# A window-attention block after a quantized convolution: spreading each head's softmax sum by a shuffle on VectorE in place of a product on TensorE

## What is computed

```python
attn = softmax(einsum('brqhd,brkhd->brhqk', qh, kh) * scale)
out  = einsum('brhqk,brkhd->brqhd', attn, vh)      # 8 channels of one head
x = x + out @ wo + bo
x = x + gelu(layernorm(x) @ w1 + bm1) @ w2 + bm2
```

## Time and profile before

| | |
|---|---|
| median of three runs | 5986.81 us (5982.99 to 5993.53) |
| profiled execution | 5993.37 us |
| its span, first to last instruction | 5991.5 us |
| PE, DVE, ACT, POOL busy | 82%, 61%, 55%, 46% |
| mean granted TensorE clock | 0.861 of full speed |

### The profile page before, as it was taken

How to read it: one execution, slowest core, us unless ns; L and a number is a source line. 1 busy time by engine, 2 the same in 40 slices (tenths; PEclk the granted TensorE clock), 3 DMA queues, 4 the chain that set the end, 5 groups by cost and what they waited for, 6 DMA issues and landing times.

```text
span 5991.5 us, 184263 instructions
## 1 busy us (share of the span) xinstructions
PE 4903.3 (82%) x43666; PEld 3154.2 (53%) x43666; DVE 3655.8 (61%) x8855; ACT 3301.0 (55%) x6282; POOL 2770.8 (46%) x9656
## 2 busy tenths in 40 slices
PE   3388888888888888888888888888887888888888
PEld 1265555545555455555555555555554555555564
DVE  2266665656656565665666666565665766656565
ACT  1156555565555655555565555655555565555646
POOL 1345444454544545444454544545444454544543
PEclk8588988989888898888888889798888989888869
DMA  2433332323323333342333323333332333323311
GB/s 64 99 91 79 88 102 61 99 73 97 88 70 106 75 88 78 86 104 60 98 74 96 90 75 100 76 88 79 86 101 64 99 73 99 88 70 102 77 24 32
DMA packets 626976, 494.17 MB, mean 82 GB/s; under 512 B 483792, under 2 KB 613968, under 8 KB 615536
## 3 DMA queue, kind: packets, MB, share of 16 engines
q10 hardware_dynamic: 335360, 212.04, 15.6%
q1 hardware_dynamic: 290416, 268.94, 15.5%
HBM read 268.80 MB, written 211.94 MB: 80 GB/s over the span
## 4 chain that ended last, share of the span: by engine, by line
PE 40%; POOL 14%; POOLq 14%; issue 14%; DMA 7%; DVE 4%; ACT 3%; DVEq 2%; ACTq 1%; SPq 1%
PE ps L984 10%; POOLq L223 9%; POOL vg L490 7%; PE ps L998 7%; PE ps L1014 6%; POOL kg L475 4%; PE ps L877 3%; DMA max_d<-tr 3%; POOLq L224 2%; POOL xin L502 2%; PE ps L897 2%; DMA qm<-qk_d 2%; DVEq L223 2%; PE ps L970 2%; PE ps L893 2%
## 5 line engine op out<-in xcount | busy, mean ns | idle before, releaser
L717 DVE TENSOR_REDUCE mx<-ps 128x4 f32<-128x1024 f32 x1568 | 1921.7, 1226 | 1763.7 <-PE ps L984 1550.6
L828 ACT ACTIVATE pt<-ps 128x512 f32<-128x512 f32 x3136 | 1695.8, 592 | 1228.5 <-PE ps L998 1145.7
L490 POOL COPY vg<-vs 64x72 f32 x6272 | 1544.2, 246 | 1396.6 <-POOL kg L475 1064.6
L984 PE MATMUL ps<-kg,qm 96*128 96x256 f32 x6272 | 1381.2, 348 | 642.5 <-POOL kg L475 224.0
L984 PEld LDWEIGHTS ps<-kg,qm 96*128 96x128 f32 x6272 | 996.3, 214 | 1437.1 <-issue 1191.2
L475 POOL CAST kg<-ks 96x128 fp32r x3136 | 858.3, 298 | 1560.5 <-POOL vg L490 926.9
L998 PE MATMUL ps<-qm,kg 97*128 97x256 f32 x6272 | 1160.0, 310 | 110.9 <-DMA qm<-max_d 56.2
L1014 PE MATMUL ps<-pt,vg 128*32 128x128 f32 x25088 | 1139.1, 304 | 38.2 <-DVE um L707 22.6
L998 PEld LDWEIGHTS ps<-qm,kg 97*128 97x128 f32 x6272 | 985.6, 215 | 156.8 <-ACT pt L828 92.5
L1014 PEld LDWEIGHTS ps<-pt,vg 128*32 128x32 f32 x25088 | 653.8, 118 | 293.1 <-issue 72.2
L626 DVE CAST kg<-ks 96x128 fp32r x3136 | 622.5, 240 | 131.7 <-issue 124.3
(11 more groups left out here) (113 smaller groups left out, 4083.8 us busy)
## 6 DMA issues: line engine op xcount, KB each, us to landing
qk_d<-stg SPq DMA_DIRECT2D x224, 448.0 KB, 3.6
qm<-qk_d ACTq DMA_DIRECT2D x1792, 42.0 KB
ks<-qk_d ACTq DMA_DIRECT2D x96, 784.0 KB, 6.2
vs<-v_d ACTq DMA_DIRECT2D x64, 882.0 KB, 7.1
xin<-in_x SPq DMA_DIRECT2D x119, 224.0 KB, 2.6
xi_d<-xi SPq DMA_DIRECT2D x112, 224.0 KB, 2.3
qk_d<-stg SPq DMA_DIRECT2D x112, 224.0 KB, 3.0
max_d<-tr SPq DMA_DIRECT2D x1568, 2.0 KB
```

The costliest lines, as they stand in the source:

```text
L490: j = pool.tensor_copy(vg[slot][rows, (k // 2) * VW:(k // 2 + 1) * VW], vs[place(m)[0]][rows, bass.ds(region, 1), :].rearrange("p o n -> p ...
L717: v.tensor_reduce(mx[h % 2][:].rearrange("p (g j e) -> p g j e", g=2, j=2)[:, :, :, 0], ps[:, 0:2, :].rearrange("p g (j k) -> p g j k", j= ...
L828: act.activation(pt[m % 2][:, c], ps[:, 2 + c, :], ACT.Exp, scale=float(HD) ** -0.5).then_inc(S["pt_ready"], 1)
L984: i = pe.matmul(ps[:, g, 256 * j:256 * j + 256], qm[c % 2][0:NP3, t, g, 2 * j:2 * j + 2, :].rearrange("p h t -> p (h t)"), kg[slot][0:NP3, ...
```

## The change

- `pick` and the products L934 go away.
- DVE shuffles instead, in `finish` at off 0 and off 1 of each strip: one STREAM_SHUFFLE of 128x448 each, which permutes rows within each group of 32. `SPREAD` gives row 16 to rows 0 to 7 and 17 to rows 8 to 15. It reads `um0`/`um1` and writes `rc`, both in on-chip memory (SBUF).
- The logarithm on ACT reads `rc` in place of the accumulators.
- PE's waits move: those that guarded banks 5 and 6 before L934 go to off 4 and off 9, or away.

```diff
--- before.py
+++ after.py
@@ -32,6 +32,8 @@
 VC = 18
 VW = 4 * VC
 
+SPREAD = [16] * HD + [17] * HD + [16] * 16
+
 
 
 
@@ -106,7 +108,6 @@
         max_d = dram("max_d", (RING, HEADS // 2, 128))
 
         ident = sb("ident", [128, 128])
-        pick = sb("pick", [128, 128])
         second = sb("second", [128, 1])
         parts = sb("parts", [128, 8])
         mean_w = sb("mean_w", [128, 128])
@@ -447,17 +448,11 @@
         def _(pool):
 
             Z = S["zero2"]
-            for i, t in enumerate((ident, pick)):
-                pool.memset(t[:], 0.0).then_inc(Z, 1)
-            pool.wait_ge(Z, 2)
+            pool.memset(ident[:], 0.0).then_inc(Z, 1)
+            pool.wait_ge(Z, 1)
             pool.affine_select(out=ident[:], in_=ident[:], compare_op=ALU.not_equal, fill=1.0, base=0,
                                pattern=[[-1, 128]], channel_multiplier=1).then_inc(Z, 1)
-            v = pick[:].rearrange("p (m b) -> p m b", m=4)
-            for e, span in ((0, slice(0, 8)), (1, slice(8, 16)), (0, slice(16, 32))):
-                w = span.stop - span.start
-                pool.affine_select(out=v[:, :, span], in_=v[:, :, span], compare_op=ALU.not_equal, fill=1.0, base=-16 - e,
-                                   pattern=[[-32, 4], [0, w]], channel_multiplier=1).then_inc(Z, 1)
-            pool.wait_ge(Z, 6)
+            pool.wait_ge(Z, 2)
             pool.sem_inc(S["const_ready"], 1)
             regs = [pool.alloc_register(f"pool_region{k}") for k in range(TOPK)]
 
@@ -677,6 +672,11 @@
                 for s, off in f_item(h):
                     n = p * NW + s
                     b = s % 2
+                    if off in (0, 1):
+                        if off == 0:
+                            v.wait_ge(S["um_ready"], p * (4 * 14) + (NW + s + 1) * 4)
+                            settled(v)
+                        v.stream_shuffle(rc[:, off], um0[:, s] if off == 0 else um1[:, b], SPREAD).then_inc(S["sum_full"], 1)
                     if off in (2, 3):
                         i = off - 2
                         v.wait_ge(S["rcs_ready"], n * 2 + i + 1)
@@ -783,7 +783,7 @@
                     if off in (1, 2):
                         i = off - 1
                         act.wait_ge(S["sum_full"], n * 2 + i + 1)
-                        act.activation(rc[:, i], ps[:, 5 + i, 0:ST], ACT.Ln).then_inc(S["lns_ready"], 1)
+                        act.activation(rc[:, i], rc[:, i], ACT.Ln).then_inc(S["lns_ready"], 1)
                         act.wait_ge(S["lns_ready"], n * 2 + i + 1)
                         act.activation(rc[:, i], rc[:, i], ACT.Exp, scale=-1.0).then_inc(S["rcs_ready"], 1)
                     if off == 6:
@@ -902,8 +902,6 @@
                 if h == ROUTE_AT:
                     pe.wait_ge(S["rx_ready"], q * NW + NW)
                     pe.wait_ge(S["l_ready"], q * (2 * NW) + 2 * NW)
-                    if not first:
-                        pe.wait_ge(S["lns_ready"], p * (2 * NW) + 1)
                     settled(pe)
                     for i in range(2):
                         d = slice(64 * i, 64 * i + 64)
@@ -921,21 +919,13 @@
 
                 for s, off in f_item(h):
                     n = p * NW + s
-                    if off == 0:
-                        pe.wait_ge(S["um_ready"], p * (4 * 14) + (NW + s + 1) * 4)
-                        if s >= 2:
-                            pe.wait_ge(S["ot_ready"], 1 + n - 1)
-                        elif kind == "loop":
-                            pe.wait_ge(S["l_ready"], (p + 2) * (2 * NW))
-                            pe.wait_ge(S["v_ready"], (p + 2) * NW)
-                        if s:
-                            pe.wait_ge(S["lnv2_ready"], n)
-                        for i, src in enumerate((um0[:, s], um1[:, s % 2])):
-                            pe.matmul(ps[:, 5 + i, 0:ST], pick[:], src, start=True, stop=True).then_inc(S["sum_full"], 1)
                     if off == 4:
                         pe.wait_ge(S["un_ready"], n * 2 + 2)
                         if s:
                             pe.wait_ge(S["z_ready"], n * 2)
+                        elif kind == "loop":
+                            pe.wait_ge(S["l_ready"], (p + 2) * (2 * NW))
+                            pe.wait_ge(S["v_ready"], (p + 2) * NW)
                         for i in range(2):
                             j = pe.matmul(ps[64 * i:64 * i + 64, 6, 0:ST], wo[:], rc[:, i], start=True, stop=True)
                         j.then_inc(S["y_full"], 1)
@@ -958,8 +948,9 @@
                         pe.matmul(ps[:, 6, 0:ST], mean_w[:], st2[:], start=True, stop=True).then_inc(S["var2_full"], 1)
                     if off == 9:
                         pe.wait_ge(S["nm2_ready"], n + 1)
-                        if s < NW - 1:
-                            pe.wait_ge(S["lns_ready"], n * 2 + 4)
+                        pe.wait_ge(S["ot_ready"], 1 + n)
+                        if s == 0 and kind == "loop":
+                            pe.wait_ge(S["lg_ready"], p + 2)
                         for i in range(2):
                             d = slice(64 * i, 64 * i + 64)
                             pe.matmul(ps[:, 5 + i, 0:ST], w1[d, 0:128], nm2[d], start=True, stop=True).then_inc(S["h_full"], 1)
```

## The result

| | before | changed |
|---|---|---|
| median, us | 5985.95 | 6012.77 |
| lowest to highest, us | 5973.4 to 5999.16 | 6001.01 to 6030.39 |
| profiled execution, us | 5993.37 | 6001.01 |
| span, us | 5991.5 | 5999.2 |
| mean granted clock | 0.861 | 0.838 |

Thirteen executions of each, side by side: the ratio is 1.0046 (1.0035 to 1.0057), so the change costs 27 us, beyond the 0.2% that can be told. The profiled execution of the changed kernel is its fastest of the thirteen and lies only 7.6 us above the one of before; for 27 us its trace alone cannot account, so a second execution of the same kernel (e5_again, span 6011.8) is read beside it.

A forecast was written before the change was run, and what follows sets the result against it. The prediction took POOL's own list to set the pace. Gains of 0 elsewhere and +7 us at 15 turns gave 6000.4 us on the profiled execution, 6.6 us above the median, so 5993 us was forecast, range 5952 to 6030.

The forecast's parts named there:

- What bounds the kernel: Whole run: steps go at POOL's pace, 3.15 us each plus quantizing, 94% of the time in which the steps run.
- Strips 0 to 5 at nothing: Strips 0 to 5 in 15 pairs: removing the products gains 0, since POOL's pace covers PE's work there.
- The shuffle: On DVE, at off 0 and off 1 of each strip: 224 shuffles, taken at 0.60 us each.
- The load of the row pattern that a rival feared: A hidden load before each shuffle, within the forecast at 0.1 us a time; part of a rival with chance 0.03.
- lock-out: Rival, chance 0.10: the shuffle keeps POOL's copies out of memory, +45 us, 6038 us.
- Strip 6: First two steps of the strip ahead of the pair's turn: gain 0.28 in the first, net +0.47 us over both.
- 15 turns: 15 x 0.47: Turns from one pair to the next: strip 6's net loss of 0.47 us at each, +7 us in all.
- POOL's waits for L998 near 129 us: Sign that the forecast is right: POOL's waits for PE's transposed scores stay near their earlier 129.0 us.
- the 2.56 and 4.39 us of the earlier trace: POOL's waits for PE at a pair's turn, 5.3 us net; 15 turns of 5 make the 76 us.
- The clock rival: Chance 0.12: thinner PE work ahead of the turn drops TensorE to 1.2 GHz, +40 us, 6033 us.
- its own condition: The clock rival decides once TensorE falls to 1.2 GHz ahead of the turn at more than five of 15 turns.
- The most likely case: Whole kernel: the forecast of 5993 us, inside the 0.2% that measurement can tell from no change, chance 0.47.

The follow-up runs named there:

- e2: The changed kernel without the shuffles as well, so neither products nor shuffles; ACT's logarithm reads a constant and waits for nobody: 1.0002 of the kernel before, 6004.72 us.
- e8: The changed kernel with the two quantizing operations moved from POOL to DVE: 0.9619 of the kernel before, 5751.51 us.
- e4: The kernel before with both shuffles added on DVE, their results unread; PE and ACT as before: 0.9984 of the kernel before, 5989.5 us.
- e1: The changed kernel with the two products and their old waits put back on PE, results unread: 0.9983 of the kernel before, 5997.68 us.
- e3: The changed kernel with the shuffle moved behind the merge L707 in DVE's list: 1.0012 of the kernel before, 6009.76 us.

## Why the prediction was right in part, and where it was wrong

**What bounds the kernel: right.** e2 (the products gone from PE, 1.0002) and e8 (the quantizing gone from POOL, 0.962) are the two sides of it. The median from `kg` to `kg` is 3.2 us as before. PE's busy share fell by one point (82% to 81%) where three were forecast, since what stays runs longer at half clock. Strips 0 to 5 at nothing: right, the steps outside the turn sum to within 1 us a pair. Of strip 0's 4.4 us of PE, 3.3 came off its first step (mean of 15) and were all given back nine steps on, as PE met POOL again.

**The shuffle: right.** 0.654 us for 0.60. The estimate scaled by columns alone from the Trainium skill ("VectorE: DVE Perf Modes", the perf-mode tier table) had been 0.53; the trace has a quarter more. The load of the row pattern that a rival feared is there but takes 7 ns. No lock-out: POOL's copies have a mean of 245 ns against 246, and four beside a shuffle took 1.16 us, below the bound of 1.3 that the prediction had set. That rival is out. The rule cited there ("SBUF — State Buffer", who interferes with whom) agrees with this.

**Strip 6: mechanism right, size off.** Forecast 2.85 and 2.95 for the two steps, measured 2.69 and 2.81: +0.15 us over the two instead of +0.47. DVE is late in place of PE in the first, and the merge waits for L833 in the second, as worked out. The sum laid durations end to end; in the rows an operation of DVE starts ahead of the recorded end of the one before: `nm` lasts 0.64 and the shuffle follows its start by 0.57, the shuffle 0.67 and `mx` 0.55, the merge 0.30 and `mx` 0.21. ACT's first part of `pt` lasts 0.58 and the second follows by 0.48. Such overlaps of some 0.1 each make up the difference.

**The step that failed: "15 turns: 15 x 0.47", and with it "POOL's waits for L998 near 129 us".** The turn was priced by the two steps that hold the edit, and everything behind was taken to move along unchanged. The waits went to 194 us, and steps 105 to 108 cost 0.8 to 1.2 us more a turn. The prediction had read the 2.56 and 4.39 us of the earlier trace rows as PE being behind by all buffers of the ring, and did not ask why it was behind. The rows above tell a part of it: small transfers behind a 784 KB one, at each load of keys. In 7 or 8 of 15 turns of the changed kernel, and in none before, PE itself waits some 2.5 us for one of them.

What is not shown is what in the change brings that wait about. It is not simply an earlier start: counted from step 17 of the pair, the first profile of the changed kernel is 1.2 us ahead of the one before at step 105, the second is level with it, and both have it. The shuffle does not make it (e2, without one, has it in 6 turns; e4 and e1, with one, in 2), so it goes with the missing products, or with PE's waits that went with them; how they bring it about stays open. e2 loses nothing by it in all, since its steps 103 and 104 are 0.87 us shorter. The low clock alone is less: in the kernel before, the five turns with half clock in the six steps take 22.1 us and the others 21.2, and e3, with 4.78 us a turn at half clock, takes 21.44 in its turns without the wait. Some 7 to 12 of the 27 us have no place of their own.

**The clock rival: half right.** It said 0.12 and +40 us. The granted clock did fall, 0.861 to 0.836, and among e1 to e4 only where the products are gone (e1, e4: 0.867; e2, e3: 0.836, 0.830). Ahead of the turn (steps 61 to 98, mean of 15) it fell from 0.858 to 0.798, less than the tenth that was to show it. But its own condition was met: in steps 103 to 108 TensorE was at half clock for over 3 us in 5 of 15 turns before, and in 12 and 14 of the changed kernel's (mean 0.948 to 0.903 and 0.891). It did not price the wait on the read back that goes with it, in which the clock fell in the pair shown. And the earlier trace rows show no idle PE at half clock: in the stretch with 0.54 it is busy for 43.51 of 47 us. Stretches of both kernels (us, busy of each engine, PEclk, DMA share, GB/s), first the changed kernel:

```profile
2966.00:3112.00 146.00, 115.97 (x1008) 74.21 (x1008) 96.03 (x244) 88.15 (x166) 77.18 (x234) 0.81 0.33 81
3112.00:3180.00 68.00, 55.48 (x467) 33.68 (x466) 39.64 (x97) 40.43 (x72) 31.23 (x121) 0.82 0.36 85
```

and the kernel before:

```profile
2969.00:3114.00 145.00, 120.94 (x1031) 75.15 (x1029) 87.44 (x213) 87.67 (x165) 76.99 (x230) 0.85 0.33 81
3114.00:3181.00 67.00, 55.76 (x468) 33.78 (x468) 38.67 (x93) 40.47 (x72) 30.02 (x119) 0.82 0.36 87
```

In this pair it fell where POOL sets the pace (0.85 to 0.81), and not over the turn as a whole (0.82 in both). The mean of 15 turns, steps 98 to 115, is 0.828 before and 0.809 and 0.800 changed. Some 285 us more at half clock, and at most 27 us more time.

**The total.** +27 us for +7, inside the range (5952 to 6030). The most likely case, within 0.2%, was wrong. The sign of the sum was right, but in part by luck: the two steps that it was made of gave 2 us, and the rest came from steps that it took to stay as they were.

## What to carry to other kernels

Price an edit not only where it stands but at the next point where the engines meet a transfer. Ask of every wait that the sum leaves alone why it is there, here a small transfer behind a large one on a fixed rhythm. And before an engine is relieved, see who waits for whom: the busiest engine here could lose 200 us for nothing, while 28 us a pair off one that was 46% busy gave 4%.

## What the runs showed of the hardware that was not expected

- The shuffle of 128 x 448 float32 within 32 rows takes 654 ns on VectorE, about a copy's 595; the load of its pattern takes 7 ns.
- A 2 KB write issued 0.96 us after a 784 KB load (3140.83 to 3141.79) had its successor 5.10 us later, one issued 0.78 us after such a load in the kernel before 5.98, against 1.68 us without a load. A small read issued 0.53 us after the load held PE up until 4.5 us after its issue; one issued 0.35 us after it held nobody up 2.65 us after its own.
- TensorE was granted half speed for 285 us more when 112 pairs of products were taken away, and with the products back and unread (e1) it ran at 0.867 and no slower than the kernel before (0.9983).
- The same quantizing operations take 1.73 and 1.35 us on GpSimd (means before, L502 and L512) and 0.37 and 0.36 us on VectorE.
